# Rounding the weights of a gated Mamba and BitLinear block: which engine and which instruction form does it

## What is computed

```python
# x: (4, 512, 512); a selective scan over ctx (4, 512, 256), gated by layernorm(x)
dt = softplus(einsum(dt_low, dt_proj_w) + dt_proj_b);  A = -exp(A_log)
def step(state, (d, b, c, u)):                  # 16 states for each of 512 channels
    state = state * exp(d * A) + (d * u) * b
    return state, sum_n(state * c)
x = x + tanh(g_xattn) * ((y + D * u) * silu(layernorm(x)))
# then a feed-forward block with quantised weights and activations
def weight_quant(w):
    scale = 1.0 / clip(mean(abs(w)), 1e-5)
    return clip(round(w * scale), -1, 1) / scale
def bitlinear(x, w): ...                        # rmsnorm, int8 rounding of x, product with weight_quant(w)
h = silu(bitlinear(x, w1)) * bitlinear(x, w2)
x = x + tanh(g_ffn) * bitlinear(h, w3)
```

## Time and profile before

| | |
|---|---|
| median of 3 runs | 718.51 us (718.45 to 718.95) |
| the profiled execution | 717.76 us |
| its span, first to last instruction | 716.0 us |
| POOL busy | 625.4 us, 87% |
| DVE busy | 605.9 us, 85% |
| ACT busy | 515.4 us, 72% |
| PE busy | 512.1 us, 72% |
| mean granted TensorE clock | 0.889 of full |

### The profile page before, as it was taken

The page is one execution under the profiler, slowest core; times in us unless marked ns, Lnnn a source line. Parts: engine busy times, 40 slices in busy tenths (PEclk is TensorE's granted clock), DMA queues, the critical chain, the costliest instruction groups (busy, mean ns, idle before and its releaser), DMA issues.

```text
span 716.0 us, 8124 instructions
## 1 busy us (share of the span) xinstructions
PE 512.1 (72%) x2562; PEld 314.2 (44%) x2562; DVE 605.9 (85%) x839; ACT 515.4 (72%) x971; POOL 625.4 (87%) x300
## 2 busy tenths in 40 slices
PE   9787889556451758787575668578686876758897
PEld 3243434223441435555353435345453544445554
DVE  7679778977999898988868888999889889888865
ACT  5844866159867868868677777898788797677653
POOL 1499999979999999999999999988998899988431
PEclk9999999969556998999785979899999998989999
DMA  4695875258950000037310000027510000000001
GB/s 169 217 402 209 305 293 211 89 181 333 413 238 15 6 29 2 29 125 266 125 61 19 31 0 16 1 82 250 197 70 6 15 2 16 0 16 16 1 16 44
DMA packets 23930, 80.78 MB, mean 113 GB/s; under 512 B 2432, under 2 KB 4608, under 8 KB 20816
## 3 DMA queue, kind: packets, MB, share of 16 engines
q1 hardware_dynamic: 23888, 80.27, 30.7%
HBM read 72.53 MB, written 7.73 MB: 112 GB/s over the span
## 4 chain that ended last, share of the span: by engine, by line
DVE 29%; ACT 21%; PE 21%; POOL 13%; issue 11%; DMA 3%; SPq 1%; DVEq 0%; ACTq 0%; POOLq 0%
DVE hh L738 7%; ACT da L708 5%; DVE hh L735 4%; POOL hh L686 4%; POOL hh L757 4%; PE bank_y L787 3%; PE bank_a L936 3%; PE bank_t L1080 3%; DMA wq<-x 2%; PE bank_b L942 2%; POOL hh L680 2%; POOL hh L752 2%; ACT room L1091 2%; DVE sm L640 2%; ACT room L977 2%
## 5 line engine op out<-in xcount | busy, mean ns | idle before, releaser
L738 DVE TENSOR_TENSOR_SCAN hh<-da,hh 128x1024 f32<-128x1024 f32 x96 | 217.5, 2277 | 6.7 <-POOL hh L686 3.5
L787 PE MATMUL bank_y<-ident,hh 128*128 128x128 f32 x1024 | 146.4, 293 | 25.0 <-POOL hh L757 19.3
L757 POOL TENSOR_TENSOR hh<-hh,cc 128x1024 f32<-128x1024 f32 x64 | 160.3, 2505 | 2.4 <-DVE hh L738 2.4
L787 PEld LDWEIGHTS bank_y<-ident,hh 128*128 128x128 f32 x1024 | 130.0, 152 | 54.9 <-POOL hh L757 27.9
L752 POOL TENSOR_TENSOR hh<-hh,cc 128x1024 f32<-128x1024 f32 x64 | 151.3, 2364 | 3.1 <-ACT hl L721 2.0
L686 POOL TENSOR_TENSOR hh<-pair,bb 128x1024 f32<-128x1024 f32 x30 | 71.6, 2388 | 26.0 <-DMA bb<-xd_scratch 25.8
L735 DVE TENSOR_TENSOR_SCAN hh<-da,hl,hh 128x256 f32<-128x256 f32 x128 | 85.0, 728 | 0.0
L680 POOL TENSOR_TENSOR hh<-wq,bb 128x1024 f32<-128x1024 f32 x32 | 75.6, 2361 | 10.7 <-PE bank_y L787 10.7
L686 POOL TENSOR_TENSOR hh<-wq,bb 128x1024 f32<-128x1024 f32 x32 | 76.6, 2395 | 3.4 <-PE bank_y L787 3.4
L680 POOL TENSOR_TENSOR hh<-pair,bb 128x1024 f32<-128x1024 f32 x32 | 75.6, 2363 | 3.4 <-PE bank_y L787 3.4
L302 PE MATMUL bank_b<-room 128*128 128x512 f32 x96 | 47.4, 640 | 24.8 <-DVE wq L406 23.2
(11 more groups left out here) (250 smaller groups left out, 1046.5 us busy)
## 6 DMA issues: line engine op xcount, KB each, us to landing
bb<-xd_scratch SPq DMA_DIRECT2D x32, 512.0 KB, 5.2
cc<-xd_scratch SPq DMA_DIRECT2D x32, 512.0 KB, 7.7
wq<-weights SPq DMA_DIRECT2D x12, 1024.0 KB, 6.5
stage<-weights SPq DMA_DIRECT2D x8, 1024.0 KB, 6.7
xin<-x SPq DMA_DIRECT2D x4, 1024.0 KB, 5.5
room<-weights SPq DMA_DIRECT2D x4, 1024.0 KB, 9.8
u_scratch<-wq SPq DMA_DIRECT2D x6, 512.0 KB, 3.4
wq<-x SPq DMA_DIRECT2D x2, 1024.0 KB, 18.5
```

Source lines behind the costliest of these rows:

```text
L738: ins = v.tensor_tensor_scan(h, flat(dbank[k % 2]), h, 0.0, ALU.mult, ALU.add)
L757: ins = g_.tensor_tensor(hh[k % NH][:, :, :], hh[k % NH][:, :, :], cc[:, s * GN:(s + 1) * GN, :], ALU.mult)
L787: mm = pe.matmul(bank_y[:, (first + c) * P:(first + c + 1) * P], flat(hh[k % NH])[:, at:at + P], ident[:, :], start=False, stop=(s == STEP ...
```

## The change

Three things change.

- `weight_round` on DVE becomes a `scalar_tensor_tensor`: it multiplies by the scale and adds a second tensor, which is one PSUM column broadcast over 2048 elements. The column is column 0 of the first row of the `da` tile that `exp(k + 4)` has just written, and the instruction first waits for that `exp`. Columns 0 of the first rows hold the magic number now, those of the second rows 0 as before. This takes four small memsets at the start in place of two.
- Pieces 1, 4, 7 and 10 are rounded by ACT (`weight_round_scalar`): an identity activation with the scale and the magic number as a bias, in the same slots 21, 25, 29 and 33. It stands in ACT's order where `weight_sign` stands, ahead of the softplus and of z. The sign of these pieces then waits for ACT itself.
- `g3d` is worked out by a `tensor_scalar` with the gate as a pointer scalar, in place of a `scalar_tensor_tensor` with two SBUF tensors.

```diff
-            WV.did(v.scalar_tensor_tensor(out=g3d, in0=wmean[:, 2:3], scalar=1.0 / 127.0, in1=gates[:, 1:2],
-                                          op0=ALU.mult, op1=ALU.mult))
+            WV.did(v.tensor_scalar(g3d, wmean[:, 2:3], gates[:, 1:2], 1.0 / 127.0, ALU.mult, ALU.mult))
...
-        def weight_round(v, i):
+        def weight_round(v, i, k):
             s = stage[round_stage(i)]
             v.wait_ge(*d_stage[round_stage(i)].of(("round", i)))
-            WV.did(v.tensor_scalar(s, s, winv[:, i // 4:i // 4 + 1], MAGIC, ALU.mult, ALU.add), ("round", i))
+            v.wait_ge(s_exp, k + 1)
+            WV.did(v.scalar_tensor_tensor(out=s, in0=s, scalar=winv[:, i // 4:i // 4 + 1],
+                                          in1=dbank[k % 2][:, 0, 0:1].to_broadcast([P, WC]),
+                                          op0=ALU.mult, op1=ALU.add), ("round", i))
+
+        def rounded_by_scalar(i):
+            return i in (1, 4, 7, 10)
+
+        def weight_round_scalar(act, i):
+            s = stage[round_stage(i)]
+            act.wait_ge(*d_stage[round_stage(i)].of(("round", i)))
+            act.wait_ge(*WV.of("gx"))
+            WA.did(act.activation(s, s, ACT.Identity, bias=magic, scale=winv[:, i // 4:i // 4 + 1]), ("round", i))
 
         def weight_sign(act, i):
-            act.wait_ge(*WV.of(("round", i)))
+            act.wait_ge(*(WA if rounded_by_scalar(i) else WV).of(("round", i)))
...
                             weight_sum(act, i)
+                        if k == round_slot(i) and rounded_by_scalar(i):
+                            weight_round_scalar(act, i)
                         if k == sign_slot(i):
                             weight_sign(act, i)
...
-                v.memset(dbank[0][:, :, 0:1], 0.0)
-                PV.did(v.memset(dbank[1][:, :, 0:1], 0.0), "zeros")
+                for bank in dbank:
+                    v.memset(bank[:, 0, 0:1], MAGIC)
+                    PV.did(v.memset(bank[:, 1, 0:1], 0.0), "zeros")
...
-                        if k == round_slot(i):
-                            weight_round(v, i)
+                        if k == round_slot(i) and not rounded_by_scalar(i):
+                            weight_round(v, i, k + LEAD)
```

## The result

The changed kernel takes 701.52 us (median of 4 runs, 699.94 to 702.73); the kernel before takes 718.48 beside it. The ratio is 0.976, with a 95% interval from 0.974 to 0.978: 2.4% faster, 17 us. A second series beside the last experiments gave 0.976 again (0.974 to 0.979). The forecast was 701.8.

The account below looks back on a forecast made before the run. POOL was taken to bound the loop from about 80 us on. Terms -2.42 - 2.77 - 11.5 = -16.7 us took the median from 718.51 to 701.8 us, with a range of 700 to 709.

Parts of the forecast that it names:

- The check that added up to 16.7 us: POOL's products from 146.43 to 233.26: the last starts 16.7 us late, equal to 2.42 + 2.77 + 11.5.
- if POOL is idle after slot 25 behind a scan or the sums: A sign named in advance that the prediction is wrong: POOL waiting after slot 25 for DVE's scan or PE's sums.
- the round's price and its port: Eight DVE rounds as scalar-tensor-tensors: 2.3 us each, with zero hold on POOL's products.
- The rival with a held POOL: Chance 0.04: eight new DVE rounds each hold POOL 2.0 us, 16 in place of 11.5, less 5.2: 717.8 us.
- -2.42 - 2.77: Terms for g3d as a tensor-scalar: POOL's waits for a scan at 146.43 and PE's sums at 158.10 go.
- -11.5: Term for the changed rounds: POOL's twelve stretched products return to normal length, 11.5 us less.
- the reading of L640 against L639: On DVE: L640 took 14.55 us, equally small L639 0.20, so g3d in L639's form would take 0.20.
- the stall isn't one of its form: Rival, chance 0.04: the new g3d waits as long as L640, only the 11.5 us goes: 707.0 us.
- the cover of 12.1 us: DVE's tolerance from L640's stall: 14.55 - 2.42 = 12.1 us of DVE lateness cost POOL nothing.
- The costs that I put at nothing under that cover: Slot 25's crowding makes ACT and DVE 3 to 6 us late, loads DVE up to 3 us: cost nothing.
- the four rounds on ACT: Four ACT activations of 1.91 us, 7.6 us more in all; ACT keeps 5.5 us left over.
- the step on slot 25: ACT has 10.9 us of work against a 4.62 us slot; the softplus product on DVE and the following scan wait.

Follow-up runs that it names:

- g3d alone: The kernel before with only g3d changed to a tensor-scalar, its twelve old rounds kept: 720.5 us, ratio 1.0032.
- the eight SBUF rounds: The changed kernel with the magic number of the eight DVE rounds read from an SBUF column in place of the PSUM column: 726.0 us, ratio 1.0108.
- g3d alone and DVE made late: The kernel before with g3d as a tensor-scalar, plus three unused reductions on DVE in slot 18: 713.7 us, ratio 0.9917.
- the probe at 95.22: The changed kernel plus five unused one-element instructions of the old g3d's form on DVE, slots 10 to 18: 716.5 us in one run.
- that at 456.98: The changed kernel plus twelve unused one-element instructions of the old g3d's form on DVE, slots 42 to 111: 715.2 us in one run.

## Why the prediction was right, point by point

*Right: POOL sets the pace, and its losses in this stretch are the gain.* The check that added up to 16.7 us, done over the whole stretch, is what carried the forecast. Measured between the same products, 130.16 to 233.26 before and 129.53 to 217.21 after, POOL needs 87.7 us in place of 103.1: 15.4. It falls short of 16.7 by the new wait of 0.97 and by a slightly longer spacing (2.32 us in place of 2.31). The sign of being wrong "if POOL is idle after slot 25 behind a scan or the sums" did come about, on a small scale: 0.97 and 0.81 us. One reading of the page was off: the slices of before stand at nine tenths from the tenth only to the 26th, the 27th and 28th read eight; nothing in the sum hangs on it.

*Right: the round's price and its port.* 2.32 us measured, 2.3 forecast, a spread of 17 ns, no product stretched (up to 2.44 us each where 2.4 was named as the bound, but 2.42 already at 120.27, before the first round). The forecast of 2.3 was a little luckier than its working: 1536 elements at its own rate of 1.1 ns are 1.7 us, not 1.6, and make 2.4. The rival with a held POOL had the right price for the same instruction with an SBUF column, 2.1 us a round, but that kernel also starved once and took 726.0 in place of the rival's 717.8.

*Wrong: that the terms belong to the edits.* "-2.42 - 2.77" was booked to g3d and "-11.5" to the rounds. Alone they give +0.3% and -0.1%. The step that failed is the reading of L640 against L639: I took starvation for a property of L640's form and turn about for one of L647's. L646 of g3d alone lasted 17.21 us, and seven of the eight SBUF rounds took turns. The change worked because it removed every instruction of the stretch that wants the port. The rival "the stall isn't one of its form" (0.04) was half true: the new g3d never waited (0.20 us), but the other form that wants the port starved as well, and in the changed kernel nothing was left for the stall to move to. The sizes of the terms were near. With g3d alone and DVE made late, no instruction starved for long and all twelve old rounds stayed: 6.0 us were gained (by the ratio), where the first two terms say 5.2, and from there to the change it is another 11.1, where the third says 11.5. (This takes the 6.7 us of added work as free, which isn't shown.)

*Wrong: the cover of 12.1 us.* It was read from POOL's wait for the one scan. It left out that DVE also feeds PE, whose sums give POOL its buffers back, and that the wait of 2.77 us behind it was the same lateness. 8.9 us of added work cost 10.5 us. The costs that I put at nothing under that cover were small but not nothing: DVE's scans run up to 8 us behind their products (scan 37 starts at 201.52, its product ended at 194.4), and POOL waits 0.97 and 0.81 us for the sums (1.03 and 1.07 in the second trace). The 0.47 us that the expectations count besides (1.14 at 313.83 in place of 0.67) isn't there in the second trace.

*Mis-sized: the four rounds on ACT.* 2.08 to 2.10 us each in place of 1.91, 8.4 in all for 7.6. It changed nothing, ACT kept up. The softplus wait of slot 25 is 3.81 us in place of 2.88, as the step on slot 25 said.

*Luck in the last microsecond.* Of the 16.3 us that the span has lost, 15.1 lie ahead of the last DVE instruction, first before, then after:

```profile
711.54 0.75 DVE L1118 SCALAR_TENSOR_TENSOR stage<-da,sm,stage 128x512 f32<-128x512 f32 x1 [2.60 <-PE da L1111]
...
696.45 0.75 DVE L1130 SCALAR_TENSOR_TENSOR stage<-da,sm,stage 128x512 f32<-128x512 f32 x1 [2.60 <-PE da L1123]
```

The other 1.2 us are the last store and its wait behind it, 2.5 us in place of 3.7. The change doesn't touch them. Without that the same sum would have missed by a good microsecond, within the run to run spread (699.9 to 702.7). Another 0.6 us stand ahead of the stretch (130.16 against 129.53), where the change has done no more than two small memsets, so they aren't its gain either.

## What to carry to other kernels

Sum the bottleneck engine's losses over a stretch, but don't divide them among edits before asking whether each would be there without the other: one loss can hide another (the stretched products hid DVE's lateness), and each edit alone can be worth nothing or less. When an instruction waits for something shared, look for the next instruction that wants it too, since the stall can move there. And read a cover from every path by which the late engine feeds the bottleneck, not from the one wait that the stall happened to show.

## What the runs showed of the hardware

A DVE instruction that reads two tensors from SBUF, or a tensor-scalar over 2048 float32 elements from and to SBUF, wants something that POOL's products hold. The Trainium skill ("SBUF — State Buffer", Who interferes with whom) calls it the shared port pair, and has the second comer blocked until the first finishes. The runs agree for most requests and not for all. Over all these traces, 42 requests of the two forms that met a running product and had to wait for it were served when it ended (waits of 0.15 to 2.3 us). Nine were not: each let at least one more product pass, and every one of them then waited for POOL's next gap, however many products that took: 14.4 to 16.0 us, over at least six more products, five times; 11.1, 6.9, 3.5 and 2.9 us once each.

What decides between turn and starvation stays open. It isn't the form or the size (one element and 2048, both forms, are on both sides), not DVE's lead (the probe at 95.22 had it and was served, that at 456.98 starved in a stretch where DVE is late), and not the first use after a pause (the early probe at 116.44 starved behind two that were served). It repeats: L640 lasted 14.55 and 14.56 us in two kernels.

One instruction form stands outside all of this: a scalar-tensor-tensor with one operand from SBUF and the other a broadcast PSUM column ran in 2.32 us eight times beside a saturated POOL, with a spread of 17 ns, and no product beside it was stretched.
